# Graph layers on one core: weight tiles loaded into the place of their low part, four places; part of the first residual sum and of its statistics taken at the end of attention

## The reference

```
x = layernorm(x + relu(h @ W_res + attention(x)))          # 12 heads
h = concat(x, node_emb[node_type])                         # 768 + 128
for w_rel, w_root, b in three layers:
    agg  = for each relation r: mean over edges of type r of h[src], times w_rel[r]
    h    = relu(agg + h @ w_root + b)
x = layernorm(x + h)
```

## Time and profile before

| | |
|---|---|
| median of three runs | 2454.03 us (2452.53 to 2455.6) |
| the profiled execution's own time | 2453.71 us |
| its span, first to last instruction | 2451.9 us |
| PE busy | 2185.7 us, 89% of the span |
| DVE busy | 1227.1 us, 50% |
| ACT busy | 785.2 us, 32% |
| POOL busy | 448.4 us, 18% |
| DMA | 215.26 MB, mean 88 GB/s |
| attention ends, graph layers begin | at 811 us of the span |

### The profile page before, as it was taken

One profiled execution on the slowest core, in us unless ns is written; L12 is line 12 of the kernel. 1 busy time (PEld: TensorE's weight loads), 2 busy tenths in 40 slices (PEclk: granted clock), 3 DMA queues, 4 the chain that ended last, 5 costly groups with the idle time before them and its releaser, 6 DMA issues.

```text
span 2451.9 us, 30026 instructions
## 1 busy us (share of the span) xinstructions
PE 2185.7 (89%) x10969; PEld 1837.1 (75%) x10970; DVE 1227.1 (50%) x1875; ACT 785.2 (32%) x1071; POOL 448.4 (18%) x369
## 2 busy tenths in 40 slices
PE   6998761888888489999999999999999899999997
PEld 2555540333333389999999899999999899999997
DVE  7887665999996542332332342332322343343335
ACT  1132332888888221121221331221211231212212
POOL 0000000899999200000000000000000000000000
PEclk8999895899999699999999999999999999999999
DMA  1133332211110343333433323333333413335332
GB/s 49 40 87 89 89 90 62 95 32 32 33 32 17 109 130 91 93 112 109 117 87 102 108 65 96 103 111 99 109 92 98 132 59 113 111 106 142 97 101 75
DMA packets 139169, 215.26 MB, mean 88 GB/s; under 512 B 87475, under 2 KB 87713, under 8 KB 139028
## 3 DMA queue, kind: packets, MB, share of 16 engines
q1 hardware_dynamic: 99921, 149.41, 21.3%
q0 software_dynamic: 38544, 62.32, 8.9%
q10 hardware_dynamic: 588, 1.92, 0.3%
HBM read 182.51 MB, written 30.70 MB: 87 GB/s over the span
## 4 chain that ended last, share of the span: by engine, by line
PE 58%; DMA 4%; DVE 3%; ACT 1%; issue 0%; ACTq 0%; DVEq 0%
PE banks L1160 30%; PE banks L1132 27%; DMA w_raw<-in_L_gnn_w_root_dram 4%; DVE w_lo L1380 1%; ACT w_hi L1262 1%; PE banks L1184 0%; PE banks L1171 0%; DVE norm_stats L1352 0%; DVE res L1348 0%; PE banks L1202 0%; DVE h_lo L1411 0%; ACT accT L1291 0%; DVE tail_stats L1431 0%; DVE back L1429 0%; ACT accT L1253 0%
## 5 line engine op out<-in xcount | busy, mean ns | idle before, releaser
L1132 PE MATMUL banks<-ct_in,h_hi 125*128 125x416 f32 (+1 forms) x1710 | 604.7, 354 | 0.6 <-ACT accT L1253 0.6
L1132 PE MATMUL banks<-ct_in,h_lo 125*128 125x416 f32 (+1 forms) x1710 | 603.5, 353 | 0.0
L1160 PE MATMUL banks<-g_hi,w_hi 128*128 128x416 f32 (+1 forms) x1440 | 516.5, 359 | 23.3 <-DVE g_lo L1402 23.3
L1160 PE MATMUL banks<-g_hi,w_lo 128*128 128x416 f32 (+1 forms) x1440 | 514.5, 357 | 0.0
L1160 PE MATMUL banks<-g_lo,w_hi 128*128 128x416 f32 (+1 forms) x1440 | 512.1, 356 | 0.0
L1380 DVE TENSOR_TENSOR w_lo<-w_raw,w_hi 128x768 fp32r<-128x768 f32 (+1 forms) x228 | 227.9, 1000 | 475.1 <-ACT w_hi L1262 475.1
L1262 ACT CAST w_hi<-w_raw 128x768 fp32r<-128x768 f32 (+1 forms) x228 | 198.0, 868 | 467.0 <-PE banks L1160 353.5
L1132 PEld LDWEIGHTS banks<-ct_in,h_lo 125*128 125x128 f32 x1710 | 323.8, 189 | 4.2
L1132 PEld LDWEIGHTS banks<-ct_in,h_hi 125*128 125x128 f32 x1710 | 322.4, 189 | 4.3 <-ACT accT L1253 0.8
L1278 ACT CAST g_hi<-gs 128x416 fp32r<-128x416 f32 (+3 forms) x180 | 97.4, 541 | 702.1 <-DVE gs L1390 702.1
L904 PE MATMUL head_sums<-pw,x 125*65 125x512 f32 x720 | 274.7, 529 | 47.9 <-POOL pw L710 33.3
(11 more groups left out here) (197 smaller groups left out, 1550.2 us busy)
## 6 DMA issues: line engine op xcount, KB each, us to landing
w_raw<-in_L_gnn_w_rel_dram SPq DMA_DIRECT2D x117, 384.0 KB, 3.1
ct_in<-s_ct POOLq DMA_DIRECT2D x18, 2031.2 KB, 27.9
w_raw<-in_L_gnn_w_rel_dram SPq DMA_DIRECT2D x54, 448.0 KB, 4.7
ct_in<-s_ct POOLq DMA_DIRECT2D x9, 2041.0 KB, 28.6
s_ct<-ct_stage SPq DMA_DIRECT2D x30, 610.4 KB
w_raw<-in_L_gnn_w_root_dram SPq DMA_DIRECT2D x39, 384.0 KB, 3.2
w_raw<-in_L_gnn_w_root_dram SPq DMA_DIRECT2D x18, 448.0 KB, 5.5
low_spread<-s_low SPq DMA_DIRECT2D x12, 610.4 KB
```

Source lines behind the costliest of these rows:

```text
L1132: ins = nc.tensor.matmul(pb[0:rows, PA, 0:s.w], a, b, start=j == 0, stop=j == len(pairs) - 1)
L1160: ins = nc.tensor.matmul(pb[:, m, 0:s.w], a, b, start=s.first and j == 0, stop=s.last and j == len(parts) - 1)
```

## The change

The weights now have four places in all. `w_raw` and `w_lo` are the same memory: a tile is loaded, ACT rounds it into `w_hi` (whose fourth place is a tensor of its own, `w_hi_last`), and DVE subtracts in place. SP's load j waits for the end of product j-4. ACT's wait on the product is now for j-4, too. The embedding rows are loaded behind load 3 rather than load 2, and the first four x1 tiles are stored behind it. In ACT's list the root of the first variance is ahead of the second w_hi.

At the end of attention, `kind_tables` stands behind the seventh y of the last head. Between the last two divisions DVE does `early(t)` for tiles 0 to 5: the sum for heads 0 to 9 and the statistics of the first half, kept in `st_e`. In the layers `first_norm` then has only heads 10 and 11 to add for these tiles and copies the six numbers; tiles 6 to 9 are as before.

```diff
+EARLY = 6
...
+            def early(t):
+                half = slice(0, HH * HD)
+                heads = res[:, t, 0:(H - 2) * HD].rearrange("p (h f) -> p h f", f=HD)
+                dve.wait_ge(res_added, H - 2)
+                nc.vector.scalar_tensor_tensor(out=heads, in0=heads, scalar=0.0, in1=x[:, t, 0:H - 2, 0:HD],
+                                               op0=ALU.max, op1=ALU.add).then_inc(early_dv, 1)
+                dve.wait_ge(early_dv, t + 1)
+                nc.vector.bn_stats(st_e[:, t], res[:, t, half])
...
                     bend_low(h * NT + s)
+                    if h == H - 1 and s == 6:
+                        kind_tables()
...
-            kind_tables()
             divide(H - 2)
+            for t in range(EARLY):
+                early(t)
             divide(H - 1)
...
-WS = 3
+WS = 4
...
-X1_STORES = {1: (0, 1), 2: (2, 3), 4: (4, 5), 6: (6, 7), 8: (8, 9)}
+X1_STORES = {3: (0, 1, 2, 3), 4: (4, 5), 6: (6, 7), 8: (8, 9)}
...
             for j, s in enumerate(W_STEPS):
-                if j >= 2:
-                    sp.wait_ge(w_lo_done, j - 1)
-                sp.dma_start(w_raw[:, j % 2, 0:s.mt * 128], weights_of(s)).then_inc(w_in[j % 2], 16)
-                if j == 2:
+                if j >= WS:
+                    sp.wait_ge(prod_done, W_STEPS[j - WS].i + 1)
+                sp.dma_start(w_raw[:, j % WS, 0:s.mt * 128], weights_of(s)).then_inc(w_in[j % WS], 16)
+                if j == 3:
                     sp.wait_ge(emb_zero, 1)
...
-                act.wait_ge(w_in[s.wi % 2], 16 * (s.wi // 2 + 1))
+                act.wait_ge(w_in[s.wi % WS], 16 * (s.wi // WS + 1))
                 if s.wi >= WS:
                     act.wait_ge(prod_done, W_STEPS[s.wi - WS].i + 1)
-                nc.scalar.copy(w_hi[:, s.wi % WS, 0:s.mt * 128], w_raw[:, s.wi % 2, 0:s.mt * 128]).then_inc(w_hi_done, 1)
+                f = slice(0, s.mt * 128)
+                nc.scalar.copy(high_of(s.wi, f), w_raw[:, s.wi % WS, f]).then_inc(w_hi_done, 1)
...
             split_w(STEPS[0])
+            root_of_variance(0)
             split_w(STEPS[1])
-            root_of_variance(0)
...
-                    heads = res[:, t].rearrange("p (h f) -> p h f", f=HD)
-                    nc.vector.scalar_tensor_tensor(out=heads, in0=heads, scalar=0.0, in1=x[:, t, :, 0:HD],
+                    h = H - 2 if t < EARLY else 0
+                    heads = res[:, t, h * HD:D].rearrange("p (h f) -> p h f", f=HD)
+                    nc.vector.scalar_tensor_tensor(out=heads, in0=heads, scalar=0.0, in1=x[:, t, h:H, 0:HD],
...
-                    for m in range(2):
-                        nc.vector.bn_stats(st[:, stage, m], res[:, t, m * 384:(m + 1) * 384]).then_inc(norm_dv, 1)
+                    if t < EARLY:
+                        nc.vector.tensor_copy(st[:, stage, 0], st_e[:, t]).then_inc(norm_dv, 1)
+                    else:
+                        nc.vector.bn_stats(st[:, stage, 0], res[:, t, 0:384]).then_inc(norm_dv, 1)
+                    nc.vector.bn_stats(st[:, stage, 1], res[:, t, 384:768]).then_inc(norm_dv, 1)
...
+        w_hi_last = t("w_hi_last", [128, D1], F32R)
+        with sb("w_raw", [128, WS, D1], F32) as w_raw:
+            pass
...
+                    w_hi, w_hi_last, w_raw, t("w_lo", [128, WS, D1], F32R),
```

More of the change, by code:

```diff
@@ L568, with attention @@
 R1_SPANS = [(286, 512), (798, N - 798), (0, 286)]
-def attention(nc, io, dram, x, res, share, oT, cols, csum, csum16, nbr, y, stored, proj_out, rows_out, node, ident):
+def attention(nc, io, dram, st_e, x, res, share, oT, cols, csum, csum16, nbr, y, stored, proj_out, rows_out, node, ident):
     a1_high, a1_low, a2_col, a_rows = cols
@@ L621, in attention @@
         o_kept = sem("o_kept"); o_turned = sem("o_turned"); denned = sem("denned"); shared = sem("shared")
-        res_added = sem("res_added")
+        res_added = sem("res_added"); early_dv = sem("early_dv")
         block = ctx.enter_context(nc.Block())
@@ L999, in halves_of_chunk, with rgcn_layers @@
     return ((s.g - 1) * 4 + at // 5, at % 5) if 0 <= at < 20 else None
-def rgcn_layers(nc, io, dram, out, ident, accT, back, emb_w, g_hi, g_lo, gs, bias, hot, hot_rows, many,
-                x, res, h_hi, h_lo, ct, w_hi, w_lo, w_raw, inv, x1_pair, x1_more):
+def rgcn_layers(nc, io, dram, st_e, out, ident, accT, back, emb_w, g_hi, g_lo, gs, bias, hot, hot_rows, many,
+                x, res, h_hi, h_lo, ct, w_hi, w_hi_last, w_raw, w_lo, inv, x1_pair, x1_more):
+    high_of = lambda wi, f: w_hi_last[:, f] if wi % WS == WS - 1 else w_hi[:, wi % WS, f]
+    low_of = lambda wi, f: w_lo[:, wi % WS, f]
     x1 = [x1_pair[:, 0], x1_pair[:, 1], accT[0:T, KX, 0:D]] + [x1_more[:, i] for i in range(NT - 5)]
@@ L1019, in rgcn_layers @@
         bias_in = sem("bias_in"); inv_in = [sem(f"inv_in{b}") for b in range(2)]
-        w_in = [sem(f"w_raw_in{b}") for b in range(2)]
+        w_in = [sem(f"w_in{b}") for b in range(WS)]
         w_hi_done = sem("w_hi_done"); w_lo_done = sem("w_lo_done")
@@ L1155, in product @@
                     else:
-                        wh, wl = w_hi[:, s.wi % WS, f], w_lo[:, s.wi % WS, f]
+                        wh, wl = high_of(s.wi, f), low_of(s.wi, f)
                         gh, gl = g_hi[:, s.gi % 2, 0:s.w], g_lo[:, s.gi % 2, 0:s.w]
@@ L1378, in split_w @@
                 dve.wait_ge(w_hi_done, s.wi + 1)
-                at = (slice(None), s.wi % WS, slice(0, s.mt * 128))
-                nc.vector.tensor_tensor(w_lo[at], w_raw[:, s.wi % 2, 0:s.mt * 128], f32(w_hi[at]), ALU.subtract).then_inc(w_lo_done, 1)
+                f = slice(0, s.mt * 128)
+                nc.vector.tensor_tensor(low_of(s.wi, f), w_raw[:, s.wi % WS, f], f32(high_of(s.wi, f)), ALU.subtract).then_inc(w_lo_done, 1)
             def scale(s):
@@ L1505, in build @@
         emb_w = t("emb_w", [128, R + 1, D1], F32R)
-        w_hi = t("w_hi", [128, WS, D1], F32R)
+        w_hi = t("w_hi", [128, WS - 1, D1], F32R)
         hot = t("hot", [T, NT, TY], F32R)
@@ L1525, in build @@
         with sb("x", [T, NT, D1], F32) as x_place:
+            st_e = x_place[:, 0:EARLY, H * (HD + 1):H * (HD + 1) + 6]
             share = x_place[:, :, D1 - HD:D1].rearrange("p (m t) f -> p m t f", m=2)
@@ L1532, in build @@
         h_lo = t("h_lo", [T, NT, D1], F32R)
-        attention(nc, io, dram, x, res, share, oT, (a1_high, a1_low, a2_col, a_rows), csum, csum16, nbr, y, stored, proj_out, rows_out, (hot, hot_rows, many), ident)
+        attention(nc, io, dram, st_e, x, res, share, oT, (a1_high, a1_low, a2_col, a_rows), csum, csum16, nbr, y, stored, proj_out, rows_out, (hot, hot_rows, many), ident)
         ct0 = t("ct_in0", [T, NT, WIDE], F32R)
@@ L1537, in build @@
         ct1 = t("ct_in1", [T, NT, WIDE], F32R)
-        rgcn_layers(nc, io, dram, out, ident, accT, back, emb_w, t("g_hi", [128, 2, WIDE], F32R), g_lo, gs, bias,
+        g_hi = t("g_hi", [128, 2, WIDE], F32R)
+        w_hi_last = t("w_hi_last", [128, D1], F32R)
+        with sb("w_raw", [128, WS, D1], F32) as w_raw:
+            pass
+        rgcn_layers(nc, io, dram, st_e, out, ident, accT, back, emb_w, g_hi, g_lo, gs, bias,
                     hot, hot_rows, many, x, res, h_hi, h_lo, (ct0, ct1),
-                    w_hi, t("w_lo", [128, WS, D1], F32R), t("w_raw", [128, 2, D1]),
+                    w_hi, w_hi_last, w_raw, t("w_lo", [128, WS, D1], F32R),
                     inv, x1_tiles, x1_more)
```

## The result

The changed kernel takes **2469.64 us**, median of six runs (2465.41 to 2475.22), against 2454.61 (2452.53 to 2455.71) for the kernel before on the same chip: ratio 1.0063, 95% interval 1.0052 to 1.0074. It is 15.0 us slower.

A forecast was written before the change was run, and what follows sets the result against it. TensorE bounds the graph layers, with 19.0 us of g_lo waits behind late weight loads. Attention +3.0, start -5.5, root steps +10.5 and SP queue +2 give +10 on 2454.03: 2464 us, range 2459 to 2472, 8 in 10 2448 to 2473.

The forecast's parts named there:

- Attention, +3.0: End of attention: moved tables make POOL late, early sums run beside its last products; +3.0 us, bounds +1 and +5.
- Start of the layers, -5.5: Layers' start: load 4 lands 42 us in, product 3 at 53.9 instead of 59.4; -5.5 us, between -2.5 and -10.5.
- First norms, 0: Residual sums of early tiles: DVE's savings vanish behind POOL's memset and the wait for load 4; 0, at most -2.
- Root group at 1200, +3.0: Root steps at 1200, 4.0 us products: gaps of 1.3, 1.4 and 1.3 us instead of 0.68; +3.0 us.
- at 1378, +1.0: Root steps at 1378 and 1389: the same milder gaps against 2.9 us of gaps before; +1.0 us.
- At 1735, +4.0: Root steps after ct_in at 1734.59: load 123 collides with it, two 3.7 us gaps, then half clock; +4.0 us.
- Change of layer, 0: Root steps from 1920 to 1955: old and new order reach product 155's end within 0.3 us; 0.
- The last root group, +2.5: Root steps from 2250 to 2276: later loads cost +2.5 us, since loads there already took 9.8 us before.
- SP queue, +2: Last layer: a load behind SP's output-store wait makes one aggregation wait; +2 us, bounds 0 and +5.
- Half clock only after 2.8 us: TensorE: a gap of about 2.8 us or more brings 3.4 us at half clock, costing 1.5 us more.
- All waits go: Rival: four places as more look-ahead remove the ten gaps and three half-clock stretches; 2428 us, chance 0.03.
- The signs: Right: g_lo waits near 28 us, POOL's last product near 804. Wrong: under ten gaps or 15 us, among others.

The follow-up runs named there:

- e5: Changed kernel with the last layer's output-tile reload, which waits for an output store, three steps later on SP's queue: 2465.37 us, ratio 1.0044.
- e4: Changed kernel with five raw and low places and three high ones, same memory, load j waiting for product j-5: 2435.73 us, ratio 0.9923.
- e1: Kernel before with only the attention part (early sums, moved tables, shorter first norms), weights as before: 2460.72 us, ratio 1.0029.
- e6: Changed kernel with the first four x1 stores issued behind load 4, the next two behind load 5: 2464.47 us, ratio 1.0042.
- e13: Changed kernel with the copy of the kept statistics written as scalar_tensor_tensor, same result: 2470.68 us, one run.
- e12: Changed kernel with five raw/low and three high places, attention as before, load 4 before stores, POOL's ct_in and inv before MEMSET and biases: 2430.33 us, ratio 0.9900.
- e14: e12 with the four 375 KB reloads for the output's tail at the change of layer eight steps later: 2418.38 us, ratio 0.9853.

## Why the prediction came out as it did

The sign, the mechanism and the range were right (2464.0 forecast, 2469.64 measured, range up to 2473). The likeliest value was 5.6 us low, and **one term carries that**: the last root group. The other terms miss by up to 1.5 us each and nearly cancel, which is luck.

- *Attention, +3.0*: 2.7 us from the last head's first product on. Right, and for the reason given: by the traces 2.35 are the tables' move (POOL late by 1.4 to 2.8 was foreseen) and 0.3 comes behind it (0 to 2.4 were put on the sums). POOL's next product starts at 792.69, foreseen 792.5. The layers begin 2.2 us later, but that time shifts by up to 3.4 us between kernels with the same attention. The Trainium skill's rule (SBUF — State Buffer, Who interferes with whom) that a DVE instruction with two SBUF inputs contends with a GpSimd instruction that reads SBUF can be seen at work, but it cost little: of the six sums of 0.81 us two took 1.64 and 2.43 beside POOL's products, which were not held (four in 10.06 us, 2.5 each), and one took 1.57 beside POOL's addition, which took 2.11 instead of 1.53. The 1.6 us that I reckoned for POOL's products did not come.

```profile
798.86 1.64 DVE L818 SCALAR_TENSOR_TENSOR res<-res,x 125x640 f32<-125x640 f32 x1
...
801.00 2.43 DVE L818 SCALAR_TENSOR_TENSOR res<-res,x 125x640 f32<-125x640 f32 x1
```

- *Start of the layers, -5.5*: -5.4, in part by luck. Load 4 lands within 0.7 us of the 42 foreseen, but from this come only 3.9 (ct_in 1 after the layers' beginning: 68.0 against 71.8). The other 1.5 is there because the first aggregation ran at half clock before and at 1.0 now, which I had not reckoned.
- *First norms, 0*: right in size. A stall was foreseen, only for the MEMSET; the bias loads ahead of it hold DVE's copy as well (5.32 us).
- *Root group at 1200, +3.0, and at 1378, +1.0*: +2.2 and -0.5. *At 1735, +4.0*: +5.5, with gaps of 4.57 and 3.55 us instead of 3.7 and 3.7. Product 122's delay of 2.50 us behind its load is as in the step; the load itself took 8.87 us and not 8.1. *Change of layer, 0*: 0.0.
- **The last root group, +2.5**: +9.1. This step failed. I priced it below the one at 1735 because its loads were slow before already, and I let the SP queue cost only where an aggregation waits (*SP queue, +2*: there it was +1.1, ahead of ct_in 25). But the queue's wait falls into the root steps: product 197 frees load 201 while SP stands behind the output store, the load then goes out 6.6 us late, where I had allowed up to 2.5, and three loads land within 5.6 us of each other after 11.9 to 14.3 us. Of the 9.1 us, 8.5 are idle time of TensorE. The queue is not even the larger part: with its wait taken away (e5) the group still costs 6.7, about half of it idle time and half the clock at 0.5. The walk of the step at 1735 should have been done for this group too, from its own landing of 9.78 us.
- *Half clock only after 2.8 us*: wrong. The 2.36 us gap at 1379.80 was followed, 1.4 us later, by 3.4 us at clock 0.50, the 2.38 us gap at 1201.49 by clock 1.00. The length of one gap does not decide it. And 3.4 us at half clock cost 1.7 us, not the 1.5 of the sum: the product at 1746.73 took 5.13 us instead of 3.45.
- *All waits go* was put at 2428 for four places more look-ahead. One load more in flight was enough: in e4 the waits for g_lo went, and the time came within 8 us of that, 2435.7; what was left is the change of layer.
- *The signs*: one of those for being wrong came up, nine gaps instead of ten, although the mechanism was right. Where I had foreseen three gaps near 1200 there was one of 2.38 us (and one of 0.25). The waits for g_lo were 33.8 us instead of 28, and POOL's last product ended at 802.7 instead of 804. Counting gaps was a poor sign; their place and the load they end on was a good one.

## What to carry to other kernels

Count look-ahead in the step whose end frees a buffer, not in buffers: "four deep" in one shared place was one step less than two raw and three split places. Count the loads that can be under way at once as well: five shared places beat two raw and three split ones by 19 us. The same eight tiles divided five and three were worth 34 us against four and four. Where one queue carries both prefetches and stores or reloads with waits of their own, write down what each prefetch stands behind at the places where its slack is smallest. Moving four reloads eight steps on gave 12 us.

## What the runs showed of the hardware

- The first 448 KB weight load took 3.1 to 3.6 us from issue to landing; behind two to four 375 KB stores on its queue and beside ct_in one took 18.1 (the changed kernel), 18.6 (e1), 24.1 (before) and 26.9 us (e4), and 7.7 with the stores behind it (e6).
- DVE's COPY and TENSOR_SCALAR stood still while POOL issued loads or filled memory, 5.32, 4.34 and 2.22 us for operations of 0.17; SCALAR_TENSOR_TENSOR, bn_stats and bn_aggr did not (e13). A bn_stats next in the list behind the held copy shows 5.24 us as well, since DVE takes its list in order. With POOL's work elsewhere the same TENSOR_SCALAR took 0.17 (e12), and the two that scale 125x768 took 1.27 us together instead of 2.55 beside the issue of ct_in (before). Not every issue holds them: in the changed kernel a TENSOR_SCALAR at 820.09 took 0.17 beside the issue of inv (819.60 to 820.18). The Trainium skill (SBUF — State Buffer, Who interferes with whom) names copy and tensor_scalar among the operations that can take the port pair shared with GpSimd; whichever of the two comes second then blocks fully. The held rows agree, and they show the wait to last over three issues and a MEMSET on end.
- A wait of TensorE that the view puts down to "issue" (7.5 us in e4, 7.9 in e12) was ACT's: it waited for a weight load ahead of the activations that TensorE needed, and it went with that load's delay (e14).
